# A dense stage turned around: the shared expert's first product with its weights stationary over 512 tokens

## The reference

```python
logits = x @ W_gate_router                      # 256 x 8
scores = sigmoid(logits)
sel    = top_k(scores + expert_bias, 2)
shared = (silu(x @ Wg_s) * (x @ Wu_s)) @ Wd_s   # 256 x 192, 256 x 192, 192 x 256
h      = silu(xr @ Wg[e]) * (xr @ Wu[e])        # the same for each token's two experts
out    = shared + sum of weights * (h @ Wd[e])
```

## Time and profile before

| | |
|---|---|
| median of 3 runs | 911.48 us (911.13 to 911.8) |
| profiled execution | 915.1 us, of which the span from the first to the last instruction is 913.4 us |
| granted TensorE clock, mean over the span | 0.958 |
| dense stage | about 335 to 477 us of the span |
| PE, DVE, ACT, POOL busy in the span | 838.2, 653.9, 474.4, 378.7 us |

### The profile page before, as it was taken

One profiled execution on the slowest core, in us unless ns is written; L12 is line 12 of the kernel. 1 busy time (PEld: TensorE's weight loads), 2 busy tenths in 40 slices (PEclk: granted clock), 3 DMA queues, 4 the chain that ended last, 5 costly groups with the idle time before them and its releaser, 6 DMA issues.

```text
span 913.4 us, 16937 instructions
## 1 busy us (share of the span) xinstructions
PE 838.2 (92%) x5115; PEld 748.6 (82%) x5115; DVE 653.9 (72%) x1917; ACT 474.4 (52%) x1006; POOL 378.7 (41%) x427
## 2 busy tenths in 40 slices
PE   7999999999999978888869999999789899988997
PEld 6879998988999867777749999999567788876776
DVE  3665677655567767787865675577677998878986
ACT  1544343243434348878625666466254344449883
POOL 2542200267000023555542444475678886323330
PEclk9899999989999987999988999999799999989999
DMA  9200000000000023433235445343411200000112
GB/s 304 106 1 2 1 1 1 1 1 1 1 1 1 1 56 114 122 106 122 79 118 148 133 117 172 95 125 119 127 47 47 92 2 1 1 1 24 47 47 70
DMA packets 48072, 58.31 MB, mean 64 GB/s; under 512 B 5616, under 2 KB 43121, under 8 KB 47985
## 3 DMA queue, kind: packets, MB, share of 16 engines
q1 hardware_dynamic: 39856, 38.85, 14.6%
q0 software_dynamic: 6480, 16.92, 5.1%
q10 hardware_dynamic: 1648, 1.46, 0.5%
HBM read 34.91 MB, written 23.22 MB: 64 GB/s over the span
## 4 chain that ended last, share of the span: by engine, by line
PE 31%; DVE 16%; issue 7%; ACT 4%; POOL 2%; SPq 1%; DMA 1%; DVEq 0%; ACTq 0%; POOLq 0%
PE bank L80 7%; PE bank L81 6%; PE bank L82 6%; PE bank L1721 2%; PE bank L1729 2%; PE bank L1620 1%; DVE xm L2110 1%; PE bank L1737 1%; DVE st L2046 1%; PE bank L1738 1%; PE bank L1741 1%; PE bank L1739 1%; PE bank L1740 1%; DVE hth L1435 1%; DMA row_tiles<-region 1%
## 5 line engine op out<-in xcount | busy, mean ns | idle before, releaser
L374 ACT CAST pth<-tp 128x512 fp32r<-128x512 f32 (+3 forms) x80 | 41.7, 525 | 128.8 <-PE tp L735 127.5
L1164 POOL DMA_INDIRECT results<-row_tiles,idu x71 | 70.0, 986 | 91.1 <-ACT row_tiles L1313 76.7
L1148 POOL DMA_INDIRECT region<-row_tiles,posu x64 | 66.3, 1036 | 59.8 <-DVE posu L1419 42.7
L559 DVE TENSOR_TENSOR ptl<-tp,pth 128x512 fp32r<-128x512 f32 (+3 forms) x80 | 48.3, 608 | 54.6 <-ACT pth L374 54.5
L80 PE MATMUL cx<-vh,pth 128*128 128x256 f32 x272 | 80.7, 297 | 1.4 <-DVE ptl L559 1.2
L82 PE MATMUL cx<-vh,ptl 128*128 128x256 f32 x272 | 76.9, 283 | 0.0
L81 PE MATMUL cx<-vl,pth 128*128 128x256 f32 x272 | 76.9, 283 | 0.0
L80 PE MATMUL sc<-hh,ph 128*128 128x512 f32 (+3 forms) x160 | 61.2, 382 | 0.3
L82 PE MATMUL sc<-hh,pl 128*128 128x512 f32 (+3 forms) x160 | 58.3, 364 | 0.0
L81 PE MATMUL sc<-hl,ph 128*128 128x512 f32 (+3 forms) x160 | 58.1, 363 | 0.0
L365 ACT ACTIVATE prob<-sc,nmx 128x512 f32<-128x512 f32 (+3 forms) x80 | 49.4, 628 | 14.0 <-DVE nmx L530 14.0
(11 more groups left out here) (430 smaller groups left out, 2802.1 us busy)
## 6 DMA issues: line engine op xcount, KB each, us to landing
row_tiles<-region SPq DMA_DIRECT2D x71, 130.0 KB, 2.4
pairs_a<-results SPq DMA_DIRECT2D x10, 512.0 KB, 4.4
x<-in_x SPq DMA_DIRECT2D x8, 512.0 KB, 8.6
out<-x SPq DMA_DIRECT2D x8, 512.0 KB, 2.9
pairs_b<-results SPq DMA_DIRECT2D x6, 512.0 KB, 4.3
early<-in_wmod SPq DMA_DIRECT2D x1, 1536.0 KB, 7.9
spare<-in_wg SPq DMA_DIRECT2D x8, 192.0 KB
spare<-in_wu SPq DMA_DIRECT2D x8, 192.0 KB
```

The lines of the kernel that those rows point to most:

```text
L374: a_.copy(pth[:, m % 2, 0:w], tp[:, m % 2, 0:w]).then_inc(s["pt_hi"], 1)
L559: vec.tensor_tensor(ptl[:, m % 2, 0:w], tp[:, m % 2, 0:w], pth[:, m % 2, 0:w], ALU.subtract).then_inc(s["pt_lo"], 1)
L1148: g_.indirect_dma_start(region, bass.IndirectOffsetOnAxis(ap=posu[:, c, t:t + 1], axis=0), hb[:, G % HB, j], None).then_inc(scattered[G % ...
L1164: g_.indirect_dma_start(results, bass.IndirectOffsetOnAxis(ap=idu[:, j % 8:j % 8 + 1], axis=0), y[:, j % YR, 0:D], None, bounds_check=KS * ...
```

## The change

The shared expert of group G is now made inside pass G, for 512 tokens at a time. `up_shared(G, m)` has 128 columns of the weights as stationary operand and hh, hl of all 512 tokens as moving operand. The 384 columns are laid out anew in HBM (`wgu_s`) as three blocks: 0 is the gate's first 128 columns, 1 the up weights' first 128, 2 the last 64 of both. So three blocks of six matmuls of 512 columns take the place of 24 matmuls of 384 columns, and the result has its features on partitions and tokens along the columns, as `down` wants its stationary operand: `turn` and the copies out of it are gone. ACT applies Silu to 512 columns twice (`gate_wide`, `gate_narrow`), DVE multiplies twice, ACT and DVE split the two results (`hid_hi`, `hid_lo`), and `shared_down(G, i)` makes two tiles at a time into both halves of `dp`, which `add(G, i)` adds in one instruction. `shared_down(G - 1, i)` and `add(G - 1, i)` stand in pass G. The next group's `turn_z`, `h_of`, `h_hi` and `h_lo` are made in pass G too. Buffers are moved so that these fit; the slot stage's semaphore counts lose the offset `N1`; POOL's `lnb` waits for the last `down`. The slot table is made behind the last pass instead of between its tiles.

```diff
@@ ACT
+            def gate_wide(G):
+                act.wait_ge(s["up_ready"], 3 * G + 1)
+                if G == 0:
+                    act.wait_ge(s["w_lo"], 2)
+                need(act, s["hid_lo"], 2 * G)
+                a_.activation(wide, up_bank[0], ACT.Silu).then_inc(s["gated"], 1)
+            def gate_narrow(G):
+                act.wait_ge(s["up_ready"], 3 * G + 2)
+                a_.activation(narrow[0:F - P], up_bank[2][0:F - P], ACT.Silu).then_inc(s["gated"], 1)
+            def hid_hi(G):
+                act.wait_ge(s["multiplied"], 2 * G + 1)
+                need(act, s["down_done"], 2 * G)
+                a_.copy(h2[0:F - P], narrow[0:F - P]).then_inc(s["hid_hi"], 1)
+                act.wait_ge(s["multiplied"], 2 * G + 2)
+                a_.copy(h1h, wide).then_inc(s["hid_hi"], 1)
...
-            z_of(1)
-            sigmoid(0)
...
-            for G in range(1, GROUPS + 1):
...
+            for G in range(GROUPS):
+                sigmoid(G)
+                if G + 1 < GROUPS:
+                    z_of(G + 1)
+                h_back(G, 0)
+                h_back(G, 1)
+                gate_wide(G)
+                up_weights(G + 1, G)
+                gate_narrow(G)
+                if G + 1 < GROUPS:
+                    h_of(G + 1)
+                hid_hi(G)
+                if G + 1 < GROUPS:
+                    h_hi(G + 1)
+                down_weights(G + 1, G)
@@ DVE
+            def multiply_narrow(G):
+                v.wait_ge(s["gated"], 2 * G + 2)
+                vec.tensor_tensor(narrow[0:F - P], narrow[0:F - P], up_bank[2][F - P:P], ALU.mult).then_inc(s["multiplied"], 1)
+            def multiply_wide(G):
+                v.wait_ge(s["up_ready"], 3 * G + 3)
+                vec.tensor_tensor(wide, wide, up_bank[1], ALU.mult).then_inc(s["multiplied"], 1)
+            def hid_lo(G):
+                v.wait_ge(s["hid_hi"], 2 * G + 1)
+                vec.tensor_tensor(h2[F - P:P], narrow[0:F - P], h2[0:F - P], ALU.subtract).then_inc(s["hid_lo"], 1)
+                v.wait_ge(s["hid_hi"], 2 * G + 2)
+                vec.tensor_tensor(h1l[:], wide, h1h, ALU.subtract).then_inc(s["hid_lo"], 1)
+            def add(G, i):
+                v.wait_ge(s["down_done"], 2 * G + i + 1)
+                a = G * GT + 2 * i
+                xt = k.x[:, a:a + 2].rearrange("p t d -> p (t d)")
+                vec.tensor_tensor(xt, xt, dp, ALU.add).then_inc(s["x_added"], 1)
...
+            for G in range(GROUPS):
+                choose(G)
+                if G:
+                    add(G - 1, 0)
+                weigh(G)
+                rank_of(G)
+                if G:
+                    add(G - 1, 1)
+                if G == GROUPS - 1:
...
+                multiply_narrow(G)
+                multiply_wide(G)
+                low_up_weights(G + 1, G)
+                hid_lo(G)
+                if G + 1 < GROUPS:
+                    h_lo(G + 1)
+                low_down_weights(G + 1, G)
@@ PE
+            def up_shared(G, m):
+                for c in range(KC):
+                    last = three(nc.tensor, up_bank[m], gsh[:, c, up_cols(m)], gsl[:, c, up_cols(m)], hh[G % 2][:, c], hl[G % 2][:, c],
+                                 c == 0, c == KC - 1)
+                last.then_inc(s["up_ready"], 1)
+            def shared_down(G, i):
+                pe.wait_ge(s["hid_lo"], 2 * G + 2)
+                need(pe, s["x_added"], 2 * G + i)
+                b = G // GPB
                 mm = nc.tensor.matmul
+                for j in range(2):
+                    q = slice((2 * i + j) * P, (2 * i + j + 1) * P)
+                    out = dp[:, j * D:(j + 1) * D]
+                    mm(out, h1h[:, q], dsh[:, b, 0], start=True, stop=False)
+                    mm(out, h1h[:, q], dsl[:, b, 0], start=False, stop=False)
+                    mm(out, h1l[:, q], dsh[:, b, 0], start=False, stop=False)
+                    mm(out, h2[:, q], dsh[:, b, 1], start=False, stop=False)
+                    last = mm(out, h2[:, q], dsl[:, b, 1], start=False, stop=True)
+                last.then_inc(s["down_done"], 1)
...
+            for G in range(GROUPS):
+                logits(G)
+                if G == 1:
+                    pe.wait_ge(s["w_lo"], 2)
+                if G:
+                    shared_down(G - 1, 0)
+                turn_h(G, 0)
+                if G:
+                    shared_down(G - 1, 1)
+                turn_h(G, 1)
+                pe.wait_ge(s["lo_h"], (G + 1) * KC)
+                if G == 0:
+                    pe.wait_ge(s["w_lo"], 1)
+                need(pe, s["gated"], 2 * G - 1)
+                up_shared(G, 0)
+                if G == 0:
+                    pe.wait_ge(s["consts"], 1)
+                count(G)
+                need(pe, s["gated"], 2 * G)
+                need(pe, s["multiplied"], 2 * G - 1)
+                up_shared(G, 2)
+                if G + 1 < GROUPS:
+                    turn_z(G + 1)
+                need(pe, s["multiplied"], 2 * G)
+                up_shared(G, 1)
```

More of the change, by code:

```diff
@@ L854, in experts_time_and_channels @@
         apart4 = sb("apart4", [P, 464])
+        table = ExitStack()
+        placing = table.enter_context(nc.sbuf_tensor("placing", [P, 3 * E * TPE + E + TPE + 2 * E + TPE + 2 + 2 * SLOTS], F32))
+        h2 = table.enter_context(nc.sbuf_tensor("h2t", [P, GW], F32R))
+        table.close()
         late = sb("late", [P, B * KC * D + KC * P + B * D])
-        there, order, mine = (late[:, i * E * TPE:(i + 1) * E * TPE].rearrange("p (t e) -> p t e", e=E) for i in range(3))
-        spot = late[:, 3 * E * TPE:3 * E * TPE + E + TPE + 2 * E + TPE + 2 + 2 * SLOTS]
+        there, order, mine = (placing[:, i * E * TPE:(i + 1) * E * TPE].rearrange("p (t e) -> p t e", e=E) for i in range(3))
+        spot = placing[:, 3 * E * TPE:]
         in_e, in_t = spot[:, 0:E], spot[:, E:E + TPE]
@@ L1465, in _ @@
                     v.sem_inc(s["fill_at"], 1)
[L1466 to L1511, removed]
-                    low_up_weights(G + 1, G)
-                    low_down_weights(G + 1, G)
-            ht_lo(N1 - 1)
-            add(N1 - 2)
-            add(N1 - 1)
+                multiply_narrow(G)
[4 more added lines that the diff above has]
+                    h_lo(G + 1)
@@ new lines, in _ @@
+                low_down_weights(G + 1, G)
+            c_.link(vec.tensor_tensor(n_e[:], base[:], ebase[:], ALU.subtract))
+            c_.link(vec.tensor_tensor(there, n_e[:].unsqueeze(1).to_broadcast([P, TPE, E]),
+                                      m128[:].unsqueeze(2).to_broadcast([P, TPE, E]), ALU.is_gt))
+            flat = lambda a: a.rearrange("p t e -> p (t e)")
+            c_.link(vec.tensor_tensor_scan(flat(order), plain[:, 0:1].to_broadcast([P, E * TPE]), flat(there), 0.0, ALU.mult, ALU.add))
@@ new lines, in _ @@
+            c_.link(vec.tensor_tensor(order, order, there, ALU.mult))
+            c_.link(vec.tensor_scalar(mine, order, own[:, 0:1], None, ALU.is_equal))
+            vec.tensor_reduce(in_e, mine.rearrange("p t e -> p e t"), AX.X, ALU.add)
+            c_.link(vec.tensor_reduce(in_t, mine, AX.X, ALU.add))
+            vec.tensor_tensor(terms[:, 0:E], in_e, iota_e[:], ALU.mult)
+            vec.tensor_tensor(terms[:, E:2 * E], in_e, by_e[:], ALU.mult)
+            c_.link(vec.tensor_tensor(terms[:, 2 * E:], in_t, by_t[:], ALU.mult))
@@ new lines, in _ @@
+            vec.tensor_reduce(found[:, 0:1], terms[:, 0:E], AX.X, ALU.add)
+            c_.link(vec.tensor_reduce(found[:, 1:2], terms[:, E:], AX.X, ALU.add))
+            vec.tensor_tensor(spread, k.ident[:, 0:SLOTS].unsqueeze(1).to_broadcast([P, 2, SLOTS]),
+                              found.unsqueeze(2).to_broadcast([P, 2, SLOTS]), ALU.mult).then_inc(s["spread"], 1)
+            add(GROUPS - 1, 0)
+            add(GROUPS - 1, 1)
+            v.wait_ge(s["slots_known"], 1)
+            vec.tensor_copy(exf[:], lg[:, 0:SLOTS])
@@ L1518, in slot_lo @@
+            vec.tensor_copy(exu[:], lg[:, 0:SLOTS])
+            c_.link(vec.tensor_scalar(colf[:], lg[:, SLOTS:2 * SLOTS], -1.0, float(USED), ALU.mult, ALU.add))
+            vec.tensor_copy(colu[:], colf[:]).then_inc(s["tabled"], 1)
             def slot_lo(p):
                 v.wait_ge(s["hi_h"], GROUPS * KC + p + 1)
-                need(v, s["gu_ready"], N1 + 2 * p - 2 if p >= 2 else 0)
+                need(v, s["gu_ready"], 2 * p - 2 if p >= 2 else 0)
                 vec.tensor_tensor(pair_of(hl, p), pair_in_bank(p), pair_of(hh, p), ALU.subtract).then_inc(s["lo_h"], 1)
@@ L1675, in _ @@
             pe.wait_ge(s["r_in"], 16)
-            logits(0)
-            pe.wait_ge(s["lo_h"], KC)
-            pe.wait_ge(s["w_lo"], 1)
-            up(0, 0, slice(0, P), None)
-            turn_z(1)
-            turn_h(0, 0)
-            pe.wait_ge(s["consts"], 1)
-            count(0)
-            turn_h(0, 1)
-            pe.wait_ge(s["w_lo"], 2)
-            for G in range(1, GROUPS + 1):
-                g, n = G - 1, (G - 1) * GT
```

(32 more changed lines are left out.)

131 lines of the change are left out of this document (37 added, 94 removed).

## The result

The changed kernel takes 927.7 us (median of four runs, 923.7 to 928.5); the kernel before took 911.6 beside it. The ratio is 1.0157 with a 95% interval of 1.0114 to 1.0200: slower by 16 us, where 8.1 were forecast, and above the range that ends at 924.0. The profiled execution is the one of 928.18 us, with a span of 926.1.

The account below looks back on a forecast made before the run. The prediction took a loop of handovers between engines as the bound: 0.6 us for passes and stage ends plus 5 x 1.5 for clock falls gave +8.1 us, 919.6 us on the 911.5 median, range 911.0 to 924.0.

Parts of the forecast that it names:

- The loop at full clock: New pass of the dense stage: the loop of waits through DVE and PE sums to 15.26 us, against 15.38 before.
- PE's own part: PE's work in the new loop, from second `shared_down` half to last `up_shared`; put at 7.5 of 15.26 us.
- The clock, five of seven passes at 1.5 us: PE's clock falls behind the thin stretch in five of seven passes, 1.5 us each.
- The bound of 1.95 for one fall: Most that one clock fall could cost a pass: 1.45 us in three rows plus at most 0.5 in a fourth.
- The rival that every pass pays in full: All passes pay for the clock, some more than one fall: 0.6 + 7 x 1.7 and more, 924 and above; chance 0.08.
- the Trainium skill's rule: Pauses between matmul bursts bring back half clock; every pass would pay, 7 x 1.5 = 10.5 us, sum +11.1.
- The first pass: First pass now holds the whole expert: 13.5 us at full clock plus 2 (0 to 3), second sigmoid at 359.5.
- the full-clock sum: First pass from its sigmoid, through `z_of`, PE and DVE, without clock loss: 13.5 us.
- The tail: Last ranks to SP's first slot load: no change from 14.6 us, between 0 and 0.9; upper bound for the table 15.5.
- The engines' work decides, 891: Rival: passes shrink to the busiest engine's work, DVE's, 12.5 us with some waits; about 20 us saved; chance 0.08.

Follow-up runs that it names:

- e1: The changed kernel plus unread 512-column matmuls in PE's two waits of each pass after the first, five behind `logits`, ten behind the first `turn_h`: 912.2 us, ratio 1.0025.
- e10: The kernel before the change plus nine unread 512-column matmuls behind its last `shared_down`: 909.0 us, ratio 0.9955 to the kernel before.
- e8: e4 plus unread matmuls in the first pass and behind the last, with slot table and slots' copies moved forward in the last group: 889.0 us, ratio 0.9752.
- e4: The changed kernel with `add(G - 1, 0)` before `choose` and unread matmuls, five behind `logits`, two behind the first `turn_h`: 895.0 us, ratio 0.9865.
- e7: The changed kernel with `shared_down`'s second half in its own bank and unread matmuls, five behind `logits`, three behind first `turn_h`: 899.8 us, ratio 0.9871.

## Why the prediction was wrong in size, and right in sign

- **The loop at full clock** (15.26 us): right, as e1 shows with 15.07 to 15.14. By its parts, summed against measured in e1: from `multiply_wide` to `choose` 4.58 against 4.79 (383.26 to 388.05), from there to the second half 3.01 against 2.77, and PE's own part 7.67 against 7.51 (390.82 to 398.33). In the kernel after the first two are 4.85 and 2.79, and PE's part is 9.09 or, in the next pass, 9.75.
- **The clock, five of seven passes at 1.5 us:** this is the step that failed. All seven stretches paid, and more each: six passes of after take 101.99 us, those of e1 90.61, and from the last `choose` (`sel`) to the last ranks (`posu`) it is 9.47 us against 7.33. Together 13.5 us instead of 7.5, which is 6.0 of the 7.9 us between forecast and result. The bound of 1.95 for one fall does not hold either: it took the low stretch to end within 4 us. Where 3.4 us of it lay on PE's part (399.5 to 402.9) that part was 1.6 us longer than in e1, where 4.9 us did (415.06 to 420.0) 2.2. The rival that every pass pays in full, given 0.08, is what happened.
- **Why five of seven.** The prediction gives no reason for its count; what it had was a trace with one visible fall in six passes. That trace could not tell what a fall costs: in e10, whose loop is that of before, the clock stood at 0.50 from 386 to 389 and from 417 to 420, and the passes around these stretches, from one `logits` to the next, still take 15.39 (382.77 to 398.16) and 15.38 us. The old loop had the slack to swallow a fall, as the prediction says of it; the new one has none. Stretches of PE in the first of these passes:

```profile
385.00:386.00 1.00, 1.00 (x8) 0.92 0.90 266
386.00:387.00 1.00, 1.00 (x4) 0.50 0.87 232
387.00:388.00 1.00, 1.00 (x5) 0.50 0.90 294
388.00:389.00 1.00, 1.00 (x7) 0.50 0.73 254
```
- **By the Trainium skill's rule** ("TensorE: Matmul & The Clock Gate", section "HAM oscillation — how this bites in real kernels"), which I had set beside my own count, each burst behind a pause starts slow again. In the kernel after that is so seven times out of seven, with 1.6 to 2.2 us for one instead of the 1.5 that I had put in. The pauses of that section are waits for DMA; here they are waits for DVE, of 1.1 to 2.5 us on PE. The one place of the trace before that I called an agreement was no pause, for PE was busy all through these rows.
- **The first pass:** 2 us for the clock, between 0 and 3. The second sigmoid came at 361.09 instead of 359.5, 3.6 us behind the full-clock sum: PEclk was 0.50 until 355, not the 0.68 of the earlier trace rows. The old order had its first wide matmuls at 343.80, the new one has them at 347.39; that this kept the clock low for longer is likely, since e8's fillings took 3.0 us off the same pass, but no run moves these matmuls alone.
- **The tail,** "no change, between 0 and 0.9": measured 0.4. (Its upper bound reads 10.8 us as the time to the end of `colu`; that is the time to its start, and 11.0 to its end. The forecast does not use it.) By the chain of waits the table is now what SP waits for last: the slot load starts 1.0 us behind the start of `colu`, where before 3.8 us lay between the two.
- **The engines' work decides, 891:** not in this change, since the add behind `choose` held PE. With that link cut and the clock held, e4, e7 and e8 have the passes of 13.2 us, near the 12.5 of this rival.

## What to carry to other kernels

Before a stage is reordered, ask which stretches of PE become thin in the new order and what stands right behind them: where a wait was on the loop here, the half clock on PE's own work behind it was paid in every pass, and the trace of an order with slack did not show the price. Cutting the wait out of the loop (two swapped lines) was worth more than filling it, and filling what was left with unread wide matmuls, in both waits and not in one, brought the rest. Size such filling to the wait, for once the clock has fallen it delays the work behind it.

## What was not expected of the hardware

The clock's low stretches in the kernel after come in two lengths: 3.4 us (399.5 to 402.9, 433.6 to 437.0) and some 10 us (409.7 to 420.0, 443.9 to 454.1), in turn until the last, which is long too. In the long ones it stays at 1.2 GHz through the second half of `shared_down` and most of the first `up_shared`, 4.9 us of work without a gap (415.06 to 420.0). Why they alternate is open. With both waits filled there was not one fall between 352 and 460 us in e1.
